# Leaving out the products of zeros around the transposes of the four norms

## The chip, the cores and the metric

The kernel runs on one core of a Trainium2 chip. The metric is the device time of one execution in microseconds, less is better. Five engines work side by side and wait for each other on semaphores: TensorE (PE in the profile, its weight loads PEld), VectorE (DVE), ScalarE (ACT), GpSimd (POOL) and SyncE (SP), which here only issues DMAs.

## What is computed

A small vision tower of two blocks on 16 images of 37 tokens (592 tokens, 256 features), all in float32. Four times a residual branch hangs on a layer norm:

```
h = tok(x)                                   # patch embedding, class token, positions
h = h + attn0(layernorm(h))                  # 16 heads, low-rank q and kv, rope, causal
h = h + moe0(layernorm(h))                   # shared expert + 2 of 8 routed experts, gelu
h = h + scan1(layernorm(h))                  # state-space scan, 16 states
h = h + moe1(layernorm(h))                   # shared + 8 of 64 routed experts, silu
layernorm(x) = (x - mean) / sqrt(var + 1e-5)
```

## The kernel before

Tokens lie on the 128 partitions, in five tiles (NTILE = 5: four of 128 rows, the last of 80). The residual h stays in SBUF. Each engine has its own program, written out by hand in the order in which it runs; only semaphores tie them. So the order on an engine is the order of the code, and no scheduler moves anything.

The four norms l = 0 to 3 all have one form, a relay between three engines:

- VectorE takes statistics of the tiles, ScalarE the square root (std), VectorE the reciprocal. Then VectorE normalizes tiles 0 and 1 (L903) and ScalarE tiles 2 and 3 (L674) into xn; the fifth tile goes through the same steps a little later.
- TensorE transposes each tile of xn in two halves of 128 columns (`transpose_xn`, L1488), waiting for each tile by `xn_landed`.
- Once the eight transposes of the first four tiles are in PSUM, VectorE (L919) and ScalarE (L679) copy them to xT, 512 columns each; the two of the fifth tile are copied by L923.
- TensorE waits for xT (`need_xT`) and multiplies it by weights: kv and q (L1528, L1532) after norm 0; the router (L1700) and the shared expert (L1718) after norm 1; the scan's projections (L1816, L1805) after norm 2; the router (L1892) and the shared experts (L1899) after norm 3.

TensorE also runs products whose result nobody reads. `keep_busy(bank, n)` (line 1478) multiplies the tile zerosb (zeros, bf16) by itself n times, 128 rows by 512 columns, into a PSUM bank that is free then. It stands in front of the transposes (16, 5 and 13 times at norms 0, 1 and 3; four single ones at norm 2, each behind a wait for a gathered tile) and, as the argument `fill` of `transpose_xn`, behind them (3, 1 and 2, 3, 3). Others stand at the kernel's start, within attention and before the first expert of the second block; the profile counts 68 by line 1481 in all. A float32 matmul that is no transpose shows in the trace as two instructions, so 10 matmuls of the program are x20 there.

The waits of the transposes and of the following matmuls are not part of `keep_busy`: a product of zeros waits for nothing but TensorE itself.

Of the kernel before, what the change touches and what calls it, by code (L numbers as in the profile page):

```python
# [22 lines left out]
NTILE = -(-NT // P)  # L23
# [62 lines left out]
def vit_tower(nc, A, out):  # L86
    ctx = ExitStack()
    with ctx:
# [285 lines left out]
        def xn_landed(eng, l, t):  # L374
            if t in (2, 3):
                eng.wait_ge(xn_act, 2 * l + t - 1)
            else:
                eng.wait_ge(xn_ready, 3 * l + (3 if t == NTILE - 1 else t + 1))
# [1096 lines left out]
        def _(pe):  # L1475
            mm = nc.tensor.matmul

            def keep_busy(bank, n):

                for _ in range(n):  # L1480
                    mm(PS[:, bank, :], zerosb[:, 0:P], zerosb[:, :], start=True, stop=True)  # L1481

            def transpose_xn(l, tiles, fill=0):
                for t in tiles:
                    xn_landed(pe, l, t)
                    for c in range(2):
                        bank, at = (XT_BANK[l] + c, t) if t < NTILE - 1 else (XT_BANK[l] + 2, c)
                        last = nc.tensor.transpose(PS[:, bank, at * P:(at + 1) * P],  # L1488
                                                   xn[:, t, c * P:(c + 1) * P], ident[:, :])
                last.then_inc(xT_mm, 1)  # L1490
                keep_busy(7, fill)
# [24 lines left out]
            pe.wait_ge(pos_in, 48)  # L1516


            keep_busy(7, 16)
            transpose_xn(0, range(NTILE - 1), 3)  # L1520
            pe.wait_ge(attn_in, 9 * 16)
            for t in range(NTILE):
                if t == 2:
# [165 lines left out]
            project_out(4)  # L1689


            keep_busy(7, 5)
            transpose_xn(1, range(NTILE - 1), 1)
            transpose_xn(1, (NTILE - 1,), 2)
            pe.wait_ge(route_in, 10 * 16)
            for t in range(NTILE):
                if t in (0, NTILE - 1):
# [99 lines left out]
                last.then_inc(late_mm, 1)  # L1797
            for t in range(1, NTILE):
                pe.wait_ge(yg_in[0][t], 16)
                keep_busy(7, 1)  # L1800
            pe.wait_ge(dtw_ready, 3)
            transpose_xn(2, range(NTILE - 1), 3)
            def make_u(c, n):
                for k in range(2):
                    last = mm(PS[:, 2 * c + n, 0:HALF], w_in[:, k, c * P:(c + 1) * P], xT[:, k, half(n)], start=k == 0, stop=k == 1)  # L1805
                return last
# [73 lines left out]
                add_to_y(hc[:, 3 + (NS - 1) % 3, :], 1, ((0, 1), (2, 3), (4,))[bank]).then_inc(yscan_mm, 1)  # L1880


            keep_busy(7, 13)
            transpose_xn(3, range(NTILE - 1), 3)
            for p, (a, b) in enumerate(ROUTER_PARTS):
                for t in range(a, b):
                    if t == 2:
# [274 lines left out]
```

## Time and profile before

| | us |
|---|---|
| median of 3 runs | 437.12 |
| lowest, highest | 436.22, 438.83 |
| the profiled execution | 437.35 |
| its span, first to last instruction | 435.7 |

The profile is of one execution. Its span is 1.65 us shorter than that execution's time; the rest lies around it. Times in the rows count from the span's start. "Granted clock" is the share of full speed that TensorE's clock had in a stretch: 1.00 is 2.4 GHz, 0.50 is 1.2 GHz. Over the whole span its mean is 0.986. The four norms lie at about 18 to 26, 102 to 106, 226 to 232 and 298 to 305 us.

### The profile page before, as it was taken

To read this page: it belongs to the slowest core of one execution; us is meant where nothing else is said; L and a number is where in the kernel's file an instruction comes from. 1 tells how busy PE (TensorE), PEld (TensorE's weight loads), DVE (VectorE), ACT (ScalarE), POOL (GpSimd) and SP (SyncE) were. 2 spreads that over 40 slices of the span, in tenths; PEclk is the share of its full clock that TensorE was granted. 3 is DMA by queue.
4 is the path that set the end of the run, shared out by engine and by line. 5 is a ranking of instruction groups with operands and counts; after the bars stand their busy time and mean duration, and the time that the engine had idled before them with its cause. 6 is when DMAs were issued, how large, how long until landed. Compare 5 with 4: busy or idle time off the path is not lost. (4 is left out here: it accounts for less than half of the span.)

```text
span 435.7 us, 8795 instructions
## 1 busy us (share of the span) xinstructions
PE 410.6 (94%) x2968; PEld 330.3 (76%) x2968; DVE 256.2 (59%) x643; ACT 140.2 (32%) x352; POOL 156.8 (36%) x129
## 2 busy tenths in 40 slices
PE   8999999979999969999999999999898999999993
PEld 5775567766779969999976499886676788888871
DVE  0548878765950111222365889997875656555545
ACT  1040068784411111111216745543311233232210
POOL 2007834540037210001470357870001256545560
PEclk9999999999999989999999799999999999999998
DMA  8764086001088577873351324321035577777463
GB/s 272 221 173 133 2 292 241 3 2 58 1 290 302 165 255 237 285 269 136 100 159 58 98 91 103 110 57 50 8 85 159 150 203 185 195 175 184 94 129 105
DMA packets 32076, 63.55 MB, mean 146 GB/s; under 512 B 6062, under 2 KB 19677, under 8 KB 29741
## 3 DMA queue, kind: packets, MB, share of 16 engines
q1 hardware_dynamic: 26381, 50.90, 37.2%
q0 software_dynamic: 5664, 12.25, 11.1%
q8 instruction: 18, 0.29, 0.3%
q14 instruction: 13, 0.11, 0.1%
HBM read 50.51 MB, written 12.63 MB: 145 GB/s over the span
## 5 line engine op out<-in xcount | busy, mean ns | idle before, releaser
L1899 PE MATMUL PS<-xT,w1s 128*128 128x296 f32 x224 | 60.7, 415 | 0.0
L1899 PEld LDWEIGHTS PS<-xT,w1s 128*128 128x128 f32 x224 | 41.4, 190 | 11.1 <-issue 0.2
L1847 PE MATMUL PS<-ident,scratch 128*128 128x128 f32 (+1 forms) x340 | 43.6, 281 | 1.2 <-DVE scratch L1286 1.1
L628 POOL DMA_INDIRECT scratch<-xg,idx_nxt x18 | 18.0, 1000 | 72.2 <-DVE idx_nxt L1420 37.8
L1280 DVE TENSOR_TENSOR_SCAN scratch<-scratch,PS 128x592 f32<-128x592 f32 x32 | 41.9, 1365 | 3.6 <-PE PS L1854 3.6
L1847 PEld LDWEIGHTS PS<-ident,scratch 128*128 128x128 f32 (+1 forms) x340 | 39.0, 184 | 5.4 <-DVE scratch L1286 2.2
L1199 DVE COPY scratch<-PS 128x144 f32<-128x144 f32 (+1 forms) x16 | 5.1, 320 | 63.2 <-PE PS L1772 63.2
L1763 PE MATMUL PS<-scratch,w0up 128*128 128x144 f32 (+1 forms) x256 | 36.9, 304 | 1.5 <-DVE scratch L1182 1.3
L1763 PEld LDWEIGHTS PS<-scratch,w0up 128*128 128x128 f32 x256 | 35.1, 194 | 3.4 <-DVE scratch L1182 2.0
L1914 PE MATMUL PS<-w1s,scratch 128*128 128x256 f32 (+1 forms) x140 | 34.8, 382 | 2.7 <-DVE scratch L1310 1.5
L783 ACT ACTIVATE scratch<-PS 128x288 f32<-128x288 f32 (+1 forms) x32 | 13.8, 431 | 69.1 <-PE PS L1763 69.1
L1772 PE MATMUL PS<-scratch,w0dn 128*128 128x144 f32 (+1 forms) x256 | 35.2, 296 | 0.0
L1772 PEld LDWEIGHTS PS<-scratch,w0dn 128*128 128x128 f32 x256 | 34.4, 190 | 0.0
L842 ACT ACTIVATE scratch<-PS 128x296 f32<-128x296 f32 x28 | 11.7, 418 | 60.3 <-PE PS L1899 60.3
L1914 PEld LDWEIGHTS PS<-w1s,scratch 128*128 128x128 f32 (+1 forms) x140 | 24.5, 182 | 8.5 <-issue 2.2
L816 ACT ACTIVATE scratch<-scratch,a_neg 128x576 f32<-128x576 f32 x32 | 24.4, 774 | 18.8 <-DVE scratch L1280 18.7
L647 POOL DMA_INDIRECT acc<-scratch,idx_cur x16 | 26.8, 1675 | 7.3 <-POOLq L623 4.9
L619 POOL TENSOR_TENSOR scratch<-scratch 128x592 f32<-128x592 f32 x15 | 25.2, 1680 | 8.8 <-DVE scratch L1280 7.3
L1323 DVE SCALAR_TENSOR_TENSOR h<-PS,gates,h 128x256 f32<-128x256 f32 (+1 forms) x60 | 25.7, 477 | 4.2 <-PE PS L1914 3.1
L1310 DVE TENSOR_TENSOR scratch<-scratch,PS 128x296 f32<-128x296 f32 x28 | 12.8, 460 | 25.4 <-ACT scratch L842 24.6
L546 POOL TENSOR_TENSOR scratch<-scratch,rsum 111x888 f32<-111x888 f32 (+1 forms) x12 | 18.1, 1506 | 23.8 <-DVE rsum L1024 23.8
L574 POOL DMA_DIRECT2D scratch<-by_expert x8 | 5.3, 661 | 56.4 <-PE PS L1747 48.6
(332 smaller groups left out, 756.1 us busy)
## 6 DMA issues: line engine op xcount, KB each, us to landing
w0dn<-in_w0dn SPq DMA_DIRECT2D x9, 1024.0 KB, 5.2
w0up<-in_w0up SPq DMA_DIRECT2D x9, 1024.0 KB, 5.2
w0dn<-in_w SPq DMA_DIRECT2D x16, 384.0 KB, 3.8
scratch<-rows_c SPq DMA_DIRECT2D x14, 296.0 KB, 3.4
by_expert<-zeros SPq DMA_DIRECT2D x2, 1920.0 KB, 13.4
w1s<-in_w SPq DMA_DIRECT2D x14, 256.0 KB, 3.1
w1s<-in_w SPq DMA_DIRECT2D x14, 128.0 KB, 3.1
w0up<-in_patchesT SPq DMA_DIRECT2D x6, 296.0 KB, 4.1
```

Of the source, the lines that this page charges most:

```text
L546: nc.gpsimd.tensor_tensor(prob[0:rows, u % PROBS, :, 0:rows], prob[0:rows, u % PROBS, :, 0:rows], rsum[0:rows, g % 2, 8 * x:8 * x + 8].uns ...
L619: nc.gpsimd.tensor_tensor(hc[:, 3 + n % 3, :], hs[:, n % 2, 1, :], cb[:, n % CROWS, :], ALU.mult).then_inc(hcp_ready, 1)
L628: nc.gpsimd.indirect_dma_start(xe1[:, half, q, :], None, xg, bass.IndirectOffsetOnAxis(ap=idx_nxt[:, q:q + 1], axis=0)).then_inc(xe1_in[q] ...
L647: nc.gpsimd.indirect_dma_start(acc[q], bass.IndirectOffsetOnAxis(ap=idx_cur[:, s, q:q + 1], axis=0), ysp[:, q, :], None, compute_op=ALU.ad ...
L816: nc.scalar.activation(barA[:, k % BA, :].rearrange("p (b t) -> p b t", b=B)[:, :, 1:T], dt[:, c, :].rearrange("p (b t) -> p b t", b=B)[:, ...
L1280: nc.vector.tensor_tensor_scan(hs[:, n % 2, c, :], barA[:, k % BA, :], IB[n % 2], 0.0, ALU.mult, ALU.add).then_inc(scanned, 1)
L1323: last = nc.vector.scalar_tensor_tensor(h[0:ROWS[t], t, :], y, gate(t), h[0:ROWS[t], t, :], ALU.mult, ALU.add)
L1763: last = mm(PS[:, z, (f % 2) * width:(f % 2 + 1) * width], w0up[:, s, c, f * P:(f + 1) * P], xeT[:, s, c, 0:width], start=c == 0, stop=c == 1)
L1772: last = mm(PS[:, 4 + c, 0:width], w0dn[:, s, f, c * P:(c + 1) * P], hTi[:, f, s * TS:s * TS + width], start=f == 0, stop=f == FT0 - 1)
L1847: last = mm(PS[0:ROWS[t], t // 2, (t % 2) * D + c * P:(t % 2) * D + (c + 1) * P], src[:, t * P:t * P + ROWS[t]], ident[:, :], start=False, ...
L1899: last = mm(PS[:, 2 * n + j, 0:HALF], w1s[:, s, w:w + F1], xT[:, c, half(n)], start=c == 0, stop=c == 1)
L1914: last = mm(PS[0:ROWS[t], out_bank(x, grp), (t % 2) * D:(t % 2 + 1) * D], hT1[:, s, t * P:t * P + ROWS[t]], w1s[:, s, 4 * F1:4 * F1 + D], ...
```

## The change

Every `keep_busy` in front of the transposes of the four norms goes, and the argument `fill` with the products behind them: 19 at norm 0, 8 at norm 1, 7 at norm 2, 16 at norm 3, 50 of 68 executed products of line 1481. The transposes, the copies, all semaphores and all waits stay, the waits for the gathered tiles at norm 2 too. No other engine's program changes.

```diff
-            keep_busy(7, 16)
-            transpose_xn(0, range(NTILE - 1), 3)
+            transpose_xn(0, range(NTILE - 1))
...
-            keep_busy(7, 5)
-            transpose_xn(1, range(NTILE - 1), 1)
-            transpose_xn(1, (NTILE - 1,), 2)
+            transpose_xn(1, range(NTILE - 1))
+            transpose_xn(1, (NTILE - 1,))
...
             for t in range(1, NTILE):
                 pe.wait_ge(yg_in[0][t], 16)
-                keep_busy(7, 1)
             pe.wait_ge(dtw_ready, 3)
-            transpose_xn(2, range(NTILE - 1), 3)
+            transpose_xn(2, range(NTILE - 1))
...
-            keep_busy(7, 13)
-            transpose_xn(3, range(NTILE - 1), 3)
+            transpose_xn(3, range(NTILE - 1))
```

TensorE's order at the first norm, before (each row: line, operation, output <- inputs, shape, how often in a row):

```order
L1505 MATMUL PS<-w0dn,w0up 80x256 x2
L1481 MATMUL PS<-zerosb 128x512 x16
L1488 MATMUL PS<-ident,xn 128x128 x8
L1481 MATMUL PS<-zerosb 128x512 x3
L1528 MATMUL PS<-wkv,xT 128x64 x4
L1488 MATMUL PS<-ident,xn 128x128 x2
L1528 MATMUL PS<-wkv,xT 128x64 x6
L1532 MATMUL PS<-xT,wq 128x296 x4
```

and the same place after the change (lines behind it count one less):

```order
L1505 MATMUL PS<-w0dn,w0up 80x256 x2
L1488 MATMUL PS<-ident,xn 128x128 x8
L1527 MATMUL PS<-wkv,xT 128x64 x4
L1488 MATMUL PS<-ident,xn 128x128 x2
L1527 MATMUL PS<-wkv,xT 128x64 x6
L1531 MATMUL PS<-xT,wq 128x296 x4
```

The embedding's last matmuls now stand right before the transposes, and the transposes right before the kv matmuls.

## Rows read from the trace of the kernel before

**Rows 1.** The page's part 1: busy us, share and instructions, TensorE.

```profile
PE 410.6 (94%) x2968; PEld 330.3 (76%) x2968; DVE 256.2 (59%) x643; ACT 140.2 (32%) x352; POOL 156.8 (36%) x129
```

**Rows 2.** Windows, TensorE: length, PE busy (matmuls), granted clock, DMA share, GB/s.

```profile
153.20:156.80 3.60, 0.00 (x0) 1.00 1.04 360
156.90:160.20 3.30, 3.30 (x16) 0.50 0.78 281
...
240.90:245.60 4.70, 3.85 (x14) 1.00 0.15 52
245.70:252.40 6.70, 6.70 (x17) 0.50 0.46 152
...
428.50:433.20 4.70, 0.00 (x0) 1.00 0.17 58
```

**Rows 3.** Waits of TensorE: who, for whom: us in total, times, longest.

```profile
PE PS L1747 <- DMA scratch<-by_expert: 3.7, 1, 3.7
...
PE PS L1914 <- DVE scratch L1310: 1.5, 2, 1.3
```

**Rows 4.** Groups by shape, L1763 on TensorE, in 156.9:160.25 and 161:166.

```profile
L1763 PE MATMUL PS<-scratch,w0up 128*128 128x144 f32 x8 | 2.2, 455 | 0.0
...
L1763 PE MATMUL PS<-scratch,w0up 128*128 128x144 f32 x21 | 2.7, 286 | 0.0
```

**Rows 5.** Timeline, first norm: start, us, engine, line, output<-inputs [idle before <-releaser].

```profile
18.48 3.62 PE L1481 MATMUL PS<-zerosb 128*128 128x512 bf16 x16
...
21.20 0.73 DVE L903 TENSOR_SCALAR xn<-h,mv,rstd 128x256 f32<-128x256 f32 x2
21.31 1.09 ACT L674 ACTIVATE xn<-h,xshift,rstd 128x256 f32<-128x256 f32 x2 [0.51 <-DVE xshift L900]
...
21.94 1.04 PE L1488 MATMUL PS<-ident,xn 128*128 128x128 f32 x8
...
23.01 0.69 DVE L919 COPY xT<-PS 128x512 f32<-128x512 f32 x1 [0.53 <-PE PS L1488]
...
23.80 1.08 PE L1528 MATMUL PS<-wkv,xT 128*128 128x64 f32 x8 [0.18 <-DVE xT L919]
...
26.23 2.21 PE L1532 MATMUL PS<-xT,wq 128*128 128x296 f32 x8
```

**Rows 6.** Timeline, second norm.

```profile
102.07 1.24 PE L1481 MATMUL PS<-zerosb 128*128 128x512 bf16 x5
...
104.50 0.41 DVE L903 TENSOR_SCALAR xn<-h,mv,rstd 128x256 f32<-128x256 f32 x1
...
104.83 0.68 DVE L919 COPY xT<-PS 128x512 f32<-128x512 f32 x1
...
105.25 0.59 PE L1481 MATMUL PS<-zerosb 128*128 128x512 bf16 x2
...
105.68 2.31 PE L1700 MATMUL PS<-rw,xT 128*128 128x8 f32 x20
...
107.84 4.23 PE L1718 MATMUL PS<-xT,w0up 128*128 128x296 f32 x16
```

**Rows 7.** Timeline, third norm.

```profile
227.71 1.03 PE L1481 MATMUL PS<-zerosb 128*128 128x512 bf16 x4
...
229.34 0.18 DVE L910 BATCH_NORM_AGGREGATE mv<-stats 128x2 f32<-128x6 f32 x1
...
229.65 0.69 DVE L919 COPY xT<-PS 128x512 f32<-128x512 f32 x1
```

**Rows 8.** Timeline, fourth norm.

```profile
298.89 2.97 PE L1481 MATMUL PS<-zerosb 128*128 128x512 bf16 x13
...
301.55 0.29 PEld L1488 LDWEIGHTS PS<-ident,xn 128*128 128x128 f32 x2 [0.19 <-DVE xn L903]
...
306.12 4.21 PE L1899 MATMUL PS<-xT,w1s 128*128 128x296 f32 x16
...
312.42 0.83 DVE L1310 TENSOR_TENSOR scratch<-scratch,PS 128x296 f32<-128x296 f32 x2
```

## The prediction

> **What bounds the kernel now.** The page first: TensorE is busy for 94% of the span [rows 1]. That share says little here, since part of it is the removed work itself. Second, the timeline around the four norms [rows 5 to 8]: each norm is a relay. VectorE and ScalarE normalize tiles into xn, TensorE transposes them, the two others copy the transposes to xT, TensorE goes on. TensorE waits there, and fills the waits with products of zeros (line 1481). Third, the granted clock over chosen stretches [rows 2]: TensorE has two levels, 2.4 GHz (1.00) and 1.2 GHz (0.50), and the windows show what it did before each fall.
>
> **What the windows say of the clock.** From 153.15 on TensorE waits 3.7 us for a DMA [rows 3]; then the clock is at 0.50 from 156.9 on for 3.3 us and a little more (3.4), though TensorE is busy throughout. The second fall comes without a long idle time: from 240.9 to 245.6 TensorE counts 3.85 of 4.7 us as busy, but its matmuls there fill 16 of the 128 rows or columns and leave a gap of 0.9 us; behind them the clock is at 0.50 for 6.7 us and a little more (6.8). Against these two, 4.7 us without a matmul at the kernel's end passed with the clock at 1.00 [rows 2]. All other waits of TensorE last 1.3 us or less [rows 3], and no fall follows them.
>
> **Price of a fall.** In the first low stretch eight matmuls of L1763 took 2.2 us, 0.28 each; behind it 21 took 2.7 us, 0.13 each [rows 4]. That is twice the time, so a low stretch costs half its length where TensorE sets the pace: 1.7 us for 3.4 us, 3.4 us for 6.8 us.
>
> **The change, part by part.** The pitch of a product of zeros is (3.62 - 2.97) / 3 = 0.217 us, from 16 in 3.62 us and 13 in 2.97 [rows 5, 8]. Taking out 50 of 68 saves 50 x 0.217 = 10.8 us of TensorE's busy time, nearly all of it inside waits. What did the zeros delay?
>
> First norm (16 ahead, 3 behind) [rows 5]. The 16 end where the transposes begin, at 21.94. VectorE has the first tile of xn at 21.20 + 0.41 = 21.6, so they start 0.3 late. But ScalarE finishes the last of the four tiles at 21.31 + 1.09 = 22.40, and its two transposes (1.04 / 8 = 0.13 each, and some way through the engine) end near 22.8 instead of 22.98. The copies to xT follow at 23.01: **-0.2 us**, passed on, since the kv and q matmuls hang on them. The three behind end before the copies do: nothing.
>
> Second norm (5 ahead, 1 and 2 behind) [rows 6]. The five delay the first transposes, but VectorE normalizes the fifth tile (104.50) ahead of its copy (104.83), so its own queue sets the copy. The last two run on until TensorE takes up L1700 at 105.68, while the copy ends at 104.83 + 0.68 = 105.51: **-0.1 us**.
>
> Third norm (4 ahead, 3 behind) [rows 7]. TensorE is dense until 227.7. The four put the transposes off by 4 x 0.217 = 0.87 us, but VectorE is occupied with the fifth tile until 229.34 + 0.18 = 229.52 and copied at 229.65: **-0.1 us**.
>
> Fourth norm (13 ahead, 3 behind) [rows 8]. The first weight load of a transpose was released by xn and not by the zeros: **0** (at most -0.15).
>
> Delays removed: -0.4 us, bounds 0 and -0.8.
>
> Now the clock. Without the zeros TensorE does, at the first norm: nothing from 18.6 to 21.6 (3.0 us), 8 transposes until 22.8, nothing for 0.8, 20 short matmuls of 64 columns with 2 transposes among them, and dense work only from 26.2 (L1532). At the second: 10 transposes and two gaps from 102.2 to 105.6, then 20 matmuls of 8 columns for 2.2 us (L1700), and dense work from 107.84 (L1718). At the third: one gap of 1.5 us between dense work (227.71 + 1.0 for the transposes to 229.65 + 0.69), hardly more than the harmless 1.3. At the fourth: nothing from 299.0 to 301.5 (2.5 us), then the row of the first norm again, dense from 306.12 (L1899). No row shows an idle time between 1.3 and 3.7 us, so the trace gives a harmless end, a harmful end, and the sparse stretch of 4.7 us that did fall. The first, second and fourth stretch are 7.6, 5.7 and 7.1 us long with half of their time in use; I hold each fall for about as likely as not, and the third norm for safe.
>
> What each costs if it falls. First: 3.4 to 6.8 us at half speed, 1.2 us of it waits for other engines: (3.4 - 1.2) / 2 = 1.1 to (6.8 - 1.2) / 2 = 2.8; I take 2.0, the middle. The kv and q matmuls pass it on whole. Second: the low stretch would lie on the dense L1718 (4.23 us for 16), and TensorE sets the pace until the experts are dispatched: 1.7 as in the first fall of the trace, bounds 0.8 and 3.4. Fourth: the router matmuls stand on the path, but L1899 has slack: it ends at 310.3, and VectorE multiplies its result only at 312.42, behind the choice of experts [rows 8]. So 0.3 to 2.0; I take 1.0. Nothing gives a delay back: the wait for the DMA at 153 ends a chain that the transposes of the first expert's rows release (POOL waits for xeT_ready), so it moves along.
>
> The Trainium skill (TensorE: Matmul & The Clock Gate, What's actually happening) says that throttled is the default state and activity releases it; the falls of rows 2 agree in kind.
>
> **Forecast (0.37): the clock falls at two of the three places.** The three pairs cost 3.7, 3.0 and 2.7, mean 3.1; less 0.4 makes +2.7. The profiled execution took 437.35 us (span 435.7), 0.2 above the median of the runs, 437.12; the difference carried to the median gives **439.8**. Its own range is 438.7 to 441.7.
>
> **Rivals.** *One fall (0.30).* For it: idle times of 3.0 and 2.5 us are shorter than the 3.7 that fell, with full transposes behind them. Mean of 2.0, 1.7 and 1.0 less 0.4 = +1.2: 438.3.
>
> *None (0.15).* The transposes and small matmuls hold the clock, as it held through 4.7 idle us at the end. Then only the -0.4 is left: 436.7. That is the other side of no change; it decides on whether the clock stays at 1.00 from 18 to 30. For more than 0.5% (2.2 us, about what a measurement of this kernel can tell) a fall of before must go away as well, the one at 156.9 or at 245.6 (1.7 or more each), for which only a shift in time speaks: 0.03.
>
> *All three (0.15).* Transposes don't hold the clock at all. Then TensorE is as good as idle from 18.6 to 23.6 (5.0 us) and from 299.0 to 303.6 (4.6), both beyond the 3.7 that fell, and from 102.2 to 105.6 with sparse work behind: 2.0 + 1.7 + 1.0 - 0.4 = +4.3: 441.4. Against it: the low stretch at 156.9 began with eight transposes and still ended after 3.4 us. The Trainium skill has this rule (TensorE: Matmul & The Clock Gate, PE-mode transpose): full clock does not engage for the transpose mode, which doesn't count as busy in the same way. No row here tests it alone.
>
> **How the numbers follow.** The likeliest case gives 439.8. The low end takes in the case of no fall (436.7, with its bound 436.5); the high end the middle of the case of three falls (442.0). Slower by over 0.5% (above 439.3): most of the forecast (0.33), a costly single fall (0.05), three falls (0.15): 0.53. Faster 0.03, within 0.44.
>
> **What the changed profile would show.** The granted clock by the microsecond around 18 to 31, 101 to 113 and 298 to 312: 0.50 in two of them, with matmuls at twice their time. Matmuls of zeros from line 1481: 18 instead of 68. The copies to xT 0.2 earlier at the first norm if the clock holds. Wrong would be: the clock at 1.00 at all norms (436.7), a fall at the third norm, or a new wait on VectorE that no clock explains. Since an execution may fall here and not there, the runs may spread more than the 2.6 us of before.

## The result: slower by 2.2%

| | before | after |
|---|---|---|
| median of 4 runs | 437.56 | 447.24 |
| lowest, highest | 436.22, 438.83 | 445.37, 449.49 |
| the profiled execution | 437.35 | 445.37 |
| its span | 435.7 | 443.7 |
| mean granted clock | 0.986 | 0.957 |

The ratio is 1.0224, with a 95% interval of 1.0184 to 1.0264. (Ratios and their intervals, here and below, leave out executions over 1.5% above the fastest of their kernel; medians and means take them in.) Without 50 products of zeros the kernel takes 9.7 us more. The forecast of 439.8 was too low, and the time is outside its range too.

The page of the changed kernel: the span, TensorE's busy time and the granted clock in 40 slices.

```profile
span 443.7 us, 8698 instructions
...
PE 410.5 (93%) x2918; PEld 333.2 (75%) x2918; DVE 256.2 (58%) x643; ACT 140.3 (32%) x352; POOL 156.4 (35%) x129
...
PEclk9959999999899799999999889999799999999998
```

TensorE's busy time is the same as before (410.5 here, 410.6 in [rows 1]), though 50 x 0.217 = 10.8 us of it were taken out. Other matmuls have grown by as much. The clock row has its first low slice (5) at 22 to 33 us, behind the first norm.

Windows of TensorE: stretch and length, busy time with its matmuls, granted clock, share of the DMA engines, GB/s. They answer to [rows 2].

```profile
18.60:21.80 3.20, 0.00 (x0) 1.00 0.60 154
21.80:23.10 1.30, 1.15 (x8) 1.00 0.81 259
23.20:33.40 10.20, 9.56 (x35) 0.50 0.65 172
112.10:115.30 3.20, 3.20 (x8) 0.50 0.00 0
149.60:156.20 6.60, 4.57 (x15) 0.50 0.63 213
236.00:240.00 4.00, 3.09 (x14) 1.00 0.30 107
252.00:258.60 6.60, 6.60 (x16) 0.50 0.41 157
305.60:308.00 2.40, 0.00 (x0) 1.00 0.01 3
308.00:309.80 1.80, 1.31 (x8) 1.00 0.44 145
310.00:316.60 6.60, 6.44 (x26) 0.50 0.14 44
```

The clock is at 0.50 behind the waits of the first norm (10.2 us), at the second (3.4), in the dispatch region (6.8), in the scan (6.8, which before has too, at 245.6) and at the fourth norm (6.8). At the third norm it stays at 1.00. The list of waits of TensorE (output, line <- releaser: us in total, times, longest) shows the transposes (L1488) waiting for xn, 7.5 us in all; before, all waits but the one for a DMA lasted 1.3 us or less [rows 3].

```profile
PE PS L1488 <- DVE xn L903: 7.5, 4, 3.5
PE PS L1780 <- DVE scratch L1199: 3.9, 1, 3.9
...
PE PS L1813 <- ACT xT L679: 1.4, 1, 1.4
```

**Where the 8.0 us of the two profiled executions arise.** The profiled execution of the changed kernel is the fastest of its four (445.37 us; the others took 1.2 to 4.1 us more), so a part of the 9.7 us has no trace to be read from. The same instruction is looked up in both traces, and the difference of its start is written down:

| instruction | before | after | difference | new here |
|---|---|---|---|---|
| first kv matmul (L1527, before L1528) | 23.80 | 23.84 | +0.04 | 0.0 |
| first of L1550 (before L1551), behind kv and q | 29.31 | 33.58 | +4.27 | +4.2 |
| last of L1639 (before L1640), end of attention | 101.14 | 105.41 | +4.27 | 0.0 |
| first of L1745 (before L1747), behind the second norm's work | 129.57 | 134.92 | +5.35 | +1.1 |
| L1761 (before L1763), fourth pair of items | 168.44 | 175.03 | +6.6 | +1.2 |
| L1813 (before L1816), behind the third norm | 230.39 | 236.91 | +6.5 | -0.1 |
| last of L1844 (before L1847), end of the scan | 296.57 | 303.06 | +6.5 | 0.0 |
| first of L1910 (before L1914), experts of the fourth norm | 312.94 | 321.11 | +8.2 | +1.7 |
| end of the span | 435.7 | 443.7 | +8.0 | -0.2 |

More than half of the loss is made in the ten microseconds behind the first norm. The timeline of the changed kernel there (start, duration, engine, line, output<-inputs, number, idle time before) answers to [rows 5]:

```profile
21.86 1.15 PE L1488 MATMUL PS<-ident,xn 128*128 128x128 f32 x8 [3.46 <-DVE xn L903]
...
23.04 0.69 DVE L919 COPY xT<-PS 128x512 f32<-128x512 f32 x1 [0.46 <-PE PS L1488]
...
23.84 1.94 PE L1527 MATMUL PS<-wkv,xT 128*128 128x64 f32 x8 [0.83 <-DVE xT L919]
...
28.45 4.26 PE L1531 MATMUL PS<-xT,wq 128*128 128x296 f32 x8
...
33.58 2.76 PE L1550 MATMUL PS<-scratch,w0up 128*128 128x296 f32 x10
```

Until 23.84 all starts agree with before within 0.1 us. Then the kv and q matmuls take twice their time. The groups by shape between 23.8 and 33.2 (busy us, mean ns) show it; in the trace of before the same groups are 2.5 us, 273 ns and 2.2 us, 419 ns:

```profile
L1527 PE MATMUL PS<-wkv,xT 128*128 128x64 f32 x20 | 4.6, 417 | 0.8 <-DVE xT L919 0.8
...
L1531 PE MATMUL PS<-xT,wq 128*128 128x296 f32 x8 | 4.3, 714 | 0.0
```

The second norm, TensorE, answers to [rows 6]: L1698 is the router (before L1700, 2.31 us), L1716 the shared expert (before L1718, 4.23 us for 16, now 5.76).

```profile
109.89 2.53 PE L1698 MATMUL PS<-rw,xT 128*128 128x8 f32 x20 [0.21 <-issue]
112.27 5.76 PE L1716 MATMUL PS<-xT,w0up 128*128 128x296 f32 x16
```

The third norm answers to [rows 7]: the copy started 6.3 us later than before, the matmul behind it 6.5, and TensorE's wait of 1.45 us had no fall behind it.

```profile
235.97 0.66 DVE L919 COPY xT<-PS 128x512 f32<-128x512 f32 x1
...
236.91 1.24 PE L1813 MATMUL PS<-xT,dt_w 128*128 128x296 f32 x4 [1.45 <-ACT xT L679]
```

The fourth norm answers to [rows 8]: L1895 (before L1899) takes 5.17 us for 16 instead of 4.21, and L1310 on VectorE comes 7.3 us later than before, at 319.72.

```profile
308.06 1.32 PE L1488 MATMUL PS<-ident,xn 128*128 128x128 f32 x8 [2.50 <-DVE xn L903]
...
310.16 1.97 PE L1888 MATMUL PS<-gw,xT 128*128 128x64 f32 x8 [0.78 <-DVE xT L919]
...
314.81 5.17 PE L1895 MATMUL PS<-xT,w1s 128*128 128x296 f32 x16
...
319.72 0.46 DVE L1310 TENSOR_TENSOR scratch<-scratch,PS 128x296 f32<-128x296 f32 x1
```

### The profile page after: what moved, and what is told of

Its sections match the earlier page's. It is cut to its first block and busy times, and to the rows that moved or that the text cites. A ratio compares the mean times of both kernels' runs of the same rounds, so it can differ in the third digit from the quotient of the medians.

```text
span 443.7 us, 8698 instructions
## 1 busy us (share of the span) xinstructions
PE 410.5 (93%) x2918; PEld 333.2 (75%) x2918; DVE 256.2 (58%) x643; ACT 140.3 (32%) x352; POOL 156.4 (35%) x129
## 5 line engine op out<-in xcount | busy, mean ns | idle before, releaser
L1895 PE MATMUL PS<-xT,w1s 128*128 128x296 f32 x224 | 61.7, 420 | 0.0
L1895 PEld LDWEIGHTS PS<-xT,w1s 128*128 128x128 f32 x224 | 42.1, 193 | 11.4 <-issue 0.7
L1844 PE MATMUL PS<-ident,scratch 128*128 128x128 f32 (+1 forms) x340 | 43.6, 281 | 1.2 <-DVE scratch L1286 1.1
L1199 DVE COPY scratch<-PS 128x144 f32<-128x144 f32 (+1 forms) x16 | 5.1, 320 | 68.6 <-PE PS L1770 64.6
L1844 PEld LDWEIGHTS PS<-ident,scratch 128*128 128x128 f32 (+1 forms) x340 | 38.8, 183 | 5.3 <-DVE scratch L1286 2.2
L1761 PE MATMUL PS<-scratch,w0up 128*128 128x144 f32 (+1 forms) x256 | 38.0, 309 | 1.3 <-DVE scratch L1182 1.0
L1761 PEld LDWEIGHTS PS<-scratch,w0up 128*128 128x128 f32 x256 | 36.2, 197 | 3.3 <-DVE scratch L1182 2.1
L1910 PE MATMUL PS<-w1s,scratch 128*128 128x256 f32 (+1 forms) x140 | 34.7, 381 | 1.3 <-DVE h L1323 1.1
L842 ACT ACTIVATE scratch<-PS 128x296 f32<-128x296 f32 x28 | 11.7, 418 | 60.2 <-PE PS L1895 60.2
L1910 PEld LDWEIGHTS PS<-w1s,scratch 128*128 128x128 f32 (+1 forms) x140 | 24.6, 182 | 6.8 <-issue 2.2
L1310 DVE TENSOR_TENSOR scratch<-scratch,PS 128x296 f32<-128x296 f32 x28 | 12.9, 461 | 25.8 <-ACT scratch L842 25.0
L546 POOL TENSOR_TENSOR scratch<-scratch,rsum 111x888 f32<-111x888 f32 (+1 forms) x12 | 18.1, 1506 | 23.8 <-DVE rsum L1024 23.8
```

What stands on the lines that cost most here:

```text
L546: nc.gpsimd.tensor_tensor(prob[0:rows, u % PROBS, :, 0:rows], prob[0:rows, u % PROBS, :, 0:rows], rsum[0:rows, g % 2, 8 * x:8 * x + 8].uns ...
L1761: last = mm(PS[:, z, (f % 2) * width:(f % 2 + 1) * width], w0up[:, s, c, f * P:(f + 1) * P], xeT[:, s, c, 0:width], start=c == 0, stop=c == 1)
L1844: last = mm(PS[0:ROWS[t], t // 2, (t % 2) * D + c * P:(t % 2) * D + (c + 1) * P], src[:, t * P:t * P + ROWS[t]], ident[:, :], start=False, ...
L1895: last = mm(PS[:, 2 * n + j, 0:HALF], w1s[:, s, w:w + F1], xT[:, c, half(n)], start=c == 0, stop=c == 1)
L1910: last = mm(PS[0:ROWS[t], out_bank(x, grp), (t % 2) * D:(t % 2 + 1) * D], hT1[:, s, t * P:t * P + ROWS[t]], w1s[:, s, 4 * F1:4 * F1 + D], ...
```

## The experiments

The theory is that the whole loss is the clock: TensorE's waits in the norms are now empty, the clock falls behind them, and the matmuls there take twice their time. The rivals: the zeros' position in the queues matters (a wait on VectorE, ScalarE or a DMA has moved), or one place alone makes it.

Every execution of a run comes with its span and mean granted clock, not only the profiled one. From these I work out a **low time** for each: 2 x span x (1 - mean granted clock), the time at 0.50 that gives this mean. A part of it costs nothing: at the end of the kernel the clock falls behind the last matmul, for the last 2.3 us of the span before and 4.1 us after. "Mean low" below is its average over a kernel's executions. Edits are against the changed kernel if nothing else is said. Means leave out two executions far outside (826 and 1442 us). The first row has the kernel before as it ran beside the others, on three chips; each ratio is to the one on the same chip (for after, to the four executions of the first table).

| kernel | n | median us | ratio to before, 95% | mean low us |
|---|---|---|---|---|
| before (three chips) | 29, 30, 29 | 436.98, 437.50, 436.34 | | 12.9, 12.4, 11.7 |
| after | 4 | 447.24 | 1.0224, 1.0184 to 1.0264 | 39.9 |
| after_again | 4 | 447.06 | 1.0233, 1.018 to 1.0286 | 39.0 |
| only_norm0 | 6 | 442.48 | 1.0109, 1.0054 to 1.0164 | 18.2 |
| only_norm1 | 12 | 440.48 | 1.0075, 1.0035 to 1.0115 | 17.5 |
| only_norm2 | 12 | 439.63 | 1.0038, 0.9996 to 1.0081 | 16.1 |
| only_norm3 | 12 | 439.60 | 1.007, 1.0025 to 1.0114 | 22.4 |
| fill_only | 4 | 440.99 | 1.0107, 1.0055 to 1.016 | 21.8 |
| no_fill | 10 | 439.05 | 1.0047, 1.0019 to 1.0076 | 15.2 |
| narrow16 | 12 | 438.29 | 1.0055, 1.0022 to 1.0089 | 14.6 |
| half_front | 10 | 438.13 | 1.0028, 0.9992 to 1.0065 | 12.6 |
| norm1_fill3 | 12 | 438.29 | 1.0026, 0.9997 to 1.0055 | 12.5 |
| scan_fill | 12 | 436.97 | 0.999, 0.9964 to 1.0017 | 10.4 |
| both_fill | 12 | 436.66 | 0.998, 0.9954 to 1.0007 | 9.1 |

A straight line through all these executions is time = 433.4 + 0.366 x low time, and they lie 0.6 us from it on average (at most 2.6). The line gives 433.4 + 0.366 x 39.9 = 448.0 for the changed kernel (measured mean 447.3). Before lies on it too: its 88 executions have 7.8 to 22.9 us of low time, and on each chip their own slope is 0.36 to 0.39. The least, 7.8 us, is a fall of 3.4 us at the dispatch and 4.4 us at the kernel's end, as in the profile of half_front.

The stretches at 0.50 in the one profile of each kernel, read in windows of 0.5 us: their length by place (the stretch at the kernel's end, which all have, is left out).

| kernel | first norm | second norm | dispatch | scan | fourth norm |
|---|---|---|---|---|---|
| before | - | - | 3.4 | 6.8 | - |
| after | 10.2 | 3.4 | 6.8 | 6.8 | 6.8 |
| after_again | 10.2 | 6.8 | 6.8 | - | 10.2 |
| only_norm0 | 6.8 | - | 3.4 | 3.4 | - |
| only_norm1 | - | 6.8 | 6.8 | - | - |
| only_norm2 | - | - | 3.4 | - | - |
| only_norm3 | - | 3.4 | 3.4 | - | 10.2 |
| fill_only | 3.4 | - | 6.8 | 6.8 | - |
| no_fill | - | 6.8 | 6.8 | 6.8 | - |
| narrow16, scan_fill, both_fill | - | 3.4 | 3.4 | - | - |
| half_front, norm1_fill3 | - | - | 3.4 | - | - |

### One norm at a time

Only one norm has lost its zeros; the three others keep theirs.

```diff
 # only_norm0: norm 0 as in the changed kernel, these put back
+            keep_busy(7, 5)
+            transpose_xn(1, range(NTILE - 1), 1)
+            transpose_xn(1, (NTILE - 1,), 2)
...
+                keep_busy(7, 1)
...
+            transpose_xn(2, range(NTILE - 1), 3)
...
+            keep_busy(7, 13)
+            transpose_xn(3, range(NTILE - 1), 3)
```

> The products of zeros are left out at the first norm only (19 of the 50). Clock theory: the granted clock falls near 24 us and stays low for 6.8 to 9.5 us, as in the changed kernel; L1551's first matmul comes 4.3 us later (29.31 to 33.6) and the kernel takes 4.3 us more, +3 to +5. Rival (each fall was chance, half of the executions): the profile may show no fall and the median is +2 at most. Rival (the time comes from the dispatch of the experts or from the DMAs, not from the clock): about 0.

Measured: +4.2 us in the mean, within the +3 to +5 expected. Windows of its TensorE at the first norm:

```profile
18.60:21.80 3.20, 0.24 (x3) 1.00 0.55 146
24.20:30.80 6.60, 6.60 (x26) 0.50 0.61 155
```

L1550 (before L1551) starts 3.3 us later than in before here (32.58), a microsecond less than the 4.3 expected. The fall appears in the four profiles of kernels without the zeros in front of the first norm (after, after_again, only_norm0, fill_only), and in none of the ten others. It lasts 10.2 us in both profiles of the changed kernel, 6.8 here and 3.4 in fill_only; whether 6.8 against 10.2 is chance, a single profile doesn't tell.

```diff
 # only_norm1: the second norm alone without zeros
+            keep_busy(7, 16)
+            transpose_xn(0, range(NTILE - 1), 3)
...
+                keep_busy(7, 1)
...
+            transpose_xn(2, range(NTILE - 1), 3)
...
+            keep_busy(7, 13)
+            transpose_xn(3, range(NTILE - 1), 3)
```

> Left out at the second norm only (8 of the 50). Clock theory: a low stretch of 3.4 us that begins within the router matmuls or the shared expert's first matmuls (107 to 112 us), +1.1 to +1.7 us. Rival by chance: +0 to +0.8 in the median. If the dispatch wait near 147 to 151 us of the changed kernel hangs on this norm, the profile shows it here: +2 more.

Measured: +2.7 us in the mean, more than the +1.1 to +1.7 expected. The clock is low for 6.8 us from 107.0, twice as long as expected, and at the dispatch it is low for 6.8 us too, as in the changed kernel:

```profile
107.00:113.50 6.50, 6.50 (x19) 0.50 0.00 1
147.80:154.40 6.60, 4.57 (x15) 0.51 0.67 212
```

That is the case of the dispatch hanging on this norm. The longer stretch there is in five of the fourteen profiles (after, after_again, only_norm1, fill_only, no_fill), and these are the kernels that lack all zeros in front of or behind the transposes of the second norm; the nine others have 3.4 us. This was noticed afterwards, and no run was made to try it. What the traces show is where the fall lies in the wait ahead of it, 3.7 to 4.5 us long in all fourteen: in the five the clock falls 1.9 to 2.2 us before the wait ends, in the nine at its end or up to 0.8 us behind it.

At the second norm itself, a fall of 3.4 us near 107 is also in the profiles of only_norm3, narrow16, scan_fill and both_fill. Of these, only_norm3 and scan_fill have the second norm as before. So the place is probably on an edge already, in before too, though its one profile has no fall there, and the change makes the falls more frequent or longer.

```diff
 # only_norm2: the third norm alone without zeros
+            keep_busy(7, 16)
+            transpose_xn(0, range(NTILE - 1), 3)
...
+            keep_busy(7, 5)
+            transpose_xn(1, range(NTILE - 1), 1)
+            transpose_xn(1, (NTILE - 1,), 2)
...
+            keep_busy(7, 13)
+            transpose_xn(3, range(NTILE - 1), 3)
```

> Left out at the third norm only (7 of the 50). Clock theory: no fall, since the gap is 1.5 us between dense work: 0, at best -0.1 us. Rival: a fall near 231 us, +1.7.

Measured: 1.0038, with an interval that just takes in 1; 0 was expected. Its profile has no fall at the third norm:

```profile
229.50:236.00 6.50, 5.10 (x25) 1.00 0.24 83
```

The prediction's "the third norm is safe" holds for every profile. A small loss in the mean (+1.6 us, at 16.1 us of low time against 12.9) is not excluded, and no trace shows where it would be.

```diff
 # only_norm3: the fourth norm alone without zeros
+            keep_busy(7, 16)
+            transpose_xn(0, range(NTILE - 1), 3)
...
+            keep_busy(7, 5)
+            transpose_xn(1, range(NTILE - 1), 1)
+            transpose_xn(1, (NTILE - 1,), 2)
...
+                keep_busy(7, 1)
...
+            transpose_xn(2, range(NTILE - 1), 3)
```

> Left out at the fourth norm only (16 of the 50). Clock theory: falls near 304 us, stays low for 6.8 us, +1.5 us (router matmuls at half speed, part of the shared expert hidden behind VectorE), up to +3. Rival by chance: under +1.

Measured: +3.0 us in the mean, twice the +1.5 expected and at its bound, and a fall behind the wait that is longer than the 6.8 us expected:

```profile
299.00:301.80 2.80, 0.46 (x5) 1.00 0.01 3
302.20:312.20 10.00, 9.21 (x36) 0.50 0.19 62
```

The four differences of means sum up to 4.2 + 2.7 + 1.6 + 3.0 = 11.5 us, with about 2 us of uncertainty on each; the whole change costs 9.7 to 9.8 in the mean. So the norms share the loss, and no place alone makes it.

### In front or behind

```diff
 # fill_only: the 38 in front stay out, the 12 behind are put back
+            transpose_xn(0, range(NTILE - 1), 3)
...
+            transpose_xn(1, range(NTILE - 1), 1)
+            transpose_xn(1, (NTILE - 1,), 2)
...
+            transpose_xn(2, range(NTILE - 1), 3)
...
+            transpose_xn(3, range(NTILE - 1), 3)
```

> The reverse: the products in front of the transposes are left out (38), those behind stay (12). Clock theory by idle time: the waits of 3.0 and 2.5 us with nothing in them still let the clock fall at the first and fourth norm, +4 to +7 us. Rival (the twelve behind suffice): within 1 us of before.

Measured: +3.4 us in the mean, below the +4 to +7 expected and above the rival's 1. First and fourth norm:

```profile
22.50:25.70 3.20, 2.98 (x14) 0.50 0.82 242
26.00:30.00 4.00, 4.00 (x27) 1.00 0.46 116
301.00:303.50 2.50, 0.40 (x4) 1.00 0.00 0
303.50:310.00 6.50, 5.90 (x38) 1.00 0.29 95
```

With three zeros behind the transposes the low stretch at the first norm is 3.4 us instead of 10.2. At the fourth norm there is none in this profile, though TensorE waited 2.5 us for xn until 303.9, as long as in the changed kernel, where a fall followed.

```diff
 # no_fill: the zeros in front as before (at all four norms), the 12 behind left out
-                keep_busy(7, fill)
...
+            keep_busy(7, 16)
+            transpose_xn(0, range(NTILE - 1), 3)
```

> Only the products behind the transposes are left out (12); those in front stay (16, 5, 4, 13). Clock theory: the gap of 0.8 us behind eight transposes that follow dense zeros is too short to let the clock fall: 0 to +1 us. Rival (the small matmuls behind are the sparse stretch that needs them): +3 to +5 us with low stretches from 26 and 306 us on.

Measured: +1.4 us in the mean, a little above the 0 to +1 expected, and no fall at the first or fourth norm in its profile (one of its slowest executions, 442.15 us). 3.4 and 1.4 make 4.8, with some 2 us of uncertainty; that is half of what the whole change costs. **The two kinds cover for each other**: without those in front the low time is 21.8 us, without those behind 15.2, and only without both is it 40.

### Is it work or the size of the work?

```diff
+            def keep_busy_narrow(bank, n):
+                for _ in range(n):
+                    mm(PS[0:16, bank, :], zerosb[:, 0:16], zerosb[:, :], start=True, stop=True)
...
+            keep_busy_narrow(7, 16)
+            transpose_xn(0, range(NTILE - 1), 3)
```

(and in the same way at the other norms and behind the transposes: all 50 are back, for the same time, on 16 of 128 columns of the array)

> All 50 products of zeros stay and last as long (512 columns each), but their weights are 16 of 128 columns of the zeros, so that they fill an eighth of the array. Theory A (what holds the clock is that TensorE has an instruction in hand): as before, 437 us. Theory B (what holds it is how much of the array works): the clock falls as in the changed kernel, 443 to 448 us, and low stretches show near 24, 107 to 112 and 303 to 310 us though TensorE counts as busy there. Rival to both (the waiting itself moves other work, the clock doesn't matter): as before, since no wait and no time slot changes.

Measured: 1.0055 (1.0022 to 1.0089), +1.4 us in the mean of all executions, against 1.0224 for the empty waits.

```profile
22.00:26.00 4.00, 3.92 (x31) 1.00 0.77 220
107.50:110.70 3.20, 3.20 (x8) 0.50 0.01 3
299.00:302.00 3.00, 3.00 (x17) 1.00 0.01 3
```

Products on an eighth of the columns (with all 128 rows) hold the clock at the first and fourth norm. They are slightly worse than full ones, as the interval leaves out 1, but their low time is 14.6 us against 12.4 with full ones and 39.9 without any. So it counts mostly that TensorE executes something, and little how much of the array that fills. This speaks against how the prediction read the fall at 245.7 (matmuls that fill 16 of 128). This run doesn't tell the clock from a rival in which the empty waits themselves move other work; that is settled by the matmuls that last twice as long and by the line through the low times above.

### The gap in the scan

```diff
 # scan_fill, against the kernel before
+            pe.wait_ge(b_c_ready, 2)
+            keep_busy(4, 4)
```

(four more products of zeros in the gap ahead of the scan's first matmuls)

> The kernel before with four more products of zeros in the wait of 0.85 us ahead of the scan's first matmuls (near 243 us), where the profile of before has the sparse stretch and the fall at 245.6. Clock theory: the fall at 245.6 becomes rare, the mean falls by 0.5 to 1.5 us, the shortest times stay. Rival (16 of 128 rows and columns are the sparse part, not the gap): the fall stays, 0; if the zeros delay the first scan, +0.3.

```profile
245.58 0.81 PE L1481 MATMUL PS<-zerosb 128*128 128x512 bf16 x3 [0.16 <-issue]
246.32 1.12 PE L1855 MATMUL PS<-scratch,sel_f 16*128 16x512 f32 x2
```

```profile
244.00:246.00 2.00, 1.84 (x8) 1.00 0.08 19
246.00:252.50 6.50, 6.50 (x33) 1.00 0.42 137
```

In this profile the gap, which lies at 245.4 to 246.3 here, is filled but for 0.16 us, and the clock stays up behind it. But of the twelve profiles whose gap is empty only five fall there (before, after, only_norm0, fill_only, no_fill), so one profile proves little; the time, 0.999 (0.9964 to 1.0017; -0.9 us in the mean, where -0.5 to -1.5 was expected), says that if the four zeros bring something, it is under 0.4%.

### The same kernel again, and how many zeros are needed

after_again is the changed kernel, unchanged, for a second profile.

> The changed kernel once more, for a second profile and more executions. Clock theory: the lost time follows the time that TensorE spends at 1.20 GHz, by about 0.37 us for each us as over the executions so far; the profile shows falls at the first norm and at one or two of the others, with lengths in steps of 3.4 us, and 447 us in the middle. Rival (the first profile was a single case, for instance in its wait at 148 to 151 us): other places, and a time that doesn't follow the clock.

Windows of its TensorE:

```profile
21.40:31.40 10.00, 8.94 (x35) 0.50 0.60 176
110.10:116.70 6.60, 6.60 (x25) 0.50 0.02 6
151.10:157.80 6.70, 4.84 (x15) 0.50 0.64 223
308.10:318.20 10.10, 9.32 (x35) 0.50 0.19 60
```

The median of 447.06 is as expected. All three falls come back, and that in the scan doesn't; those of the second and fourth norm are longer, and that of the first norm comes earlier: it begins before the transposes, which take 1.94 us instead of 1.15. The places are the kernel's; their lengths (3.4, 6.8 or 10.2 us) differ from execution to execution.

```diff
 # half_front: half of those in front
+            keep_busy(7, 8)
+            transpose_xn(0, range(NTILE - 1), 3)
...
+            keep_busy(7, 2)
+            transpose_xn(1, range(NTILE - 1), 1)
+            transpose_xn(1, (NTILE - 1,), 2)
...
+                keep_busy(7, 1 if t < 3 else 0)
...
+            transpose_xn(2, range(NTILE - 1), 3)
...
+            keep_busy(7, 7)
+            transpose_xn(3, range(NTILE - 1), 3)
```

> The products in front of the transposes are halved (16 to 8, 5 to 2, 4 to 2, 13 to 7), those behind stay. Clock theory by idle time: the longest wait with nothing in it is 1.3 us, as the harmless ones of before, so within 1 us of before. Rival (a wait must be filled to its end): +2 to +3.5 us, as with none in front.

```profile
22.00:26.00 4.00, 3.82 (x30) 1.00 0.86 257
299.00:302.00 3.00, 2.00 (x13) 1.00 0.17 56
302.00:308.00 6.00, 5.86 (x37) 1.00 0.23 74
```

19 of the 38 in front leave waits of a microsecond or so (1.3 us the longest) and, in the profile, no fall at the norms: 1.0028 (0.9992 to 1.0065), +0.9 us in the mean, within the 1 us expected. So the number was generous, and the step from half to none is the dear one.

norm1_fill3 and both_fill try the other direction on the kernel before, with three zeros instead of one behind the second norm's first eight transposes, the second with the four of scan_fill too.

```diff
 # norm1_fill3 (and both_fill, which adds the two lines of scan_fill)
-            transpose_xn(1, range(NTILE - 1), 1)
+            transpose_xn(1, range(NTILE - 1), 3)
```

> The kernel before with 3 instead of 1 product behind the first eight transposes of the second norm, where TensorE waits 0.57 us longer. Three profiles with that norm untouched show a fall at 106.6 to 107.5 us. Clock theory: that fall becomes rarer, mean -0.3 to -1 us. Rival (it comes from the matmuls of 8 columns behind, not from the gap): 0.

> The kernel before with both additions, four products ahead of the scan and two more at the second norm. Clock theory: the gains add, mean -1 to -2 us, the executions of 440 us and more become rare, the shortest times stay at 435 us. Rival: no change beyond that of the scan's four alone (-0.8).

Measured: norm1_fill3 1.0026 (0.9997 to 1.0055), both_fill 0.998 (0.9954 to 1.0007). In the means that is +0.6 us, where -0.3 to -1 was expected, and -0.7 us, where -1 to -2 was. Neither differs from before by more than a measurement can tell, so no gain is shown. What both_fill does show is a narrower spread: 435.11 to 437.90 over 12 executions, at 9.1 us of low time, where before went from 435.56 to 442.15 beside it. It is no faster at its best, it has fewer bad executions, and that much rests on 12.

## Why the prediction was wrong

**Right.** What changes is the clock, at the norms; the copies and transposes stay in their places, and the loss is read from matmuls at twice their time. The third norm, with a gap of 1.45 us where 1.5 was expected, stayed at full speed in all profiles. Slower had the greatest chance.

**How many falls.** "I hold each fall for about as likely as not" was the first step that failed, and with it the forecast of two falls. The case of all three had 0.15 and is the one that came: at the first, second and fourth norm, in both profiles of the changed kernel, and all eight of its executions have 34 to 44 us of low time. The bracket was 1.3 us harmless, 3.7 us harmful, and between them I chose a coin. The waits came out at 3.5 us (first norm, where I had 3.0) and 2.5 (fourth); the first was close to the harmful end, with thin work behind, and should have weighed more. The 4.7 us at the kernel's end with the clock still up [rows 2] were taken as evidence for a chip that forgives; a low stretch begins there too, at 433.4, right behind that window.

**The size of the sum.** The number of falls is the smaller part of the miss. The prediction's own case of three falls is +4.3 (441.4), and the two profiled executions differ by 8.0. Against its terms the first norm cost 2.3 more, the dispatch, which had no term, 1.2, the fourth norm 0.7, the second 0.6 less, and the 0.4 for delays didn't show. The range had no room for this: it ended at 442.0, there called the middle of a case whose sum is 441.4, while the upper bounds of its three terms (2.8, 3.4 and 2.0) reach 445.3.

**The first norm's term.** 2.0, with bounds of 1.1 and 2.8; it measured 4.3. The bounds took the two lengths that the trace of before had, 3.4 and 6.8, and here the clock stayed low for 10.2 us. The longest row of another place was no upper bound. The work behind the wait may be the reason (at 156.9 dense matmuls followed, here transposes, 20 kv matmuls of 64 columns and another wait), but that isn't shown: with the same work behind it the fall of only_norm0 lasted 6.8. (10.2 - 1.2) / 2 = 4.5 would have been the sum with the measured length. It was visible in the trace of before that its one low stretch behind sparse work was the long one, 6.8.

**The second and fourth.** 1.7 for the second: it measured 1.7 at the end of L1716 (118.03 against 112.07, less the 4.3 from before it), of which 1.1 was left at 134.9. 1.0 for the fourth: 1.7 at L1910, 1.5 at the end. Both are within their bounds.

**A place that wasn't in the sum.** The low stretch behind the dispatch, 3.4 us in [rows 2], is 6.8 in both profiles of the changed kernel. Across it the delay grows by 1.2. The wait there has another position in the program than in [rows 3]: 3.9 us behind VectorE's L1199, ahead of the second pair of items, instead of 3.7 for a DMA at L1747, ahead of the third. All profiles but that of before have this other wait, those with a span of 434.6 and 434.7 too (half_front, norm1_fill3, only_norm2), so it costs nothing by itself. The low stretch is 6.8 instead of 3.4 us where the clock falls within the wait and not at its end, as said at only_norm1; why it falls earlier in some kernels stays open. Filling this wait with zeros was not tried.

**The delays removed, -0.4.** They don't show: the first kv matmul starts at 23.84 against 23.80. VectorE's xn came 0.1 later in this execution (L903 at 21.30, before 21.20 [rows 5]), and with it the rest. At the other norms the clock covers so small a term.

**The rule on transposes.** The eight transposes at 21.9 to 23.1 ran with the clock at 1.00 and did not keep it there. The rule of the Trainium skill (TensorE: Matmul & The Clock Gate, PE-mode transpose), named with the case of three falls, is compatible with that. But the wait of 3.5 us ahead of them may be enough by itself, and no run here put other work of the same length in their place, so the rule itself is not shown; in the one profile of fill_only the fall was shorter with three zeros behind them.

**Sums of low time.** (39.9 - 12.5) x 0.366 = 10.0 us, against 9.7 measured. The factor is 0.366 and not 0.5; where TensorE waits within a low stretch, or another engine sets the pace, the low clock costs nothing. At the first norm the factor is 4.3 / 10.2 = 0.42.

## What to carry to other kernels

A wait of some microseconds on TensorE that is filled with useless products is not idle time to be saved: ask what clock the next matmuls get, and take the price from low stretches that follow work as sparse as yours, not from the shortest in the trace. When such fillers are trimmed, halving them and looking again is cheap, while removing both groups at once can cost more than the two losses together (here 9.7 us against 4.8). To judge such an edit, compare the mean granted clock of many executions: one profile shows one outcome of several.

## What the runs showed of the hardware

- Products on 16 of 128 columns held the clock nearly as well as full ones: 14.6 us of low time on average, against 12.4 for before and 39.9 without any.
- An unchanged kernel has 7.8 to 22.9 us of low time from execution to execution, and its time, 435.0 to 443.7 us, goes with it, by 0.36 to 0.39 us for each.
- Waits of TensorE of 3.5 us (first norm) and 2.5 us (fourth) with sparse work behind had 6.8 to 10.2 us at half clock after them in the changed kernel; 1.45 us at the third norm between dense work had none.
- In the wait of about 4 us at the dispatch, a fall 1.9 to 2.2 us before its end went with 6.8 us at half clock (five profiles), one at its end or just behind it with 3.4 us (nine).
